# Four layers of a small convolution net on one core: two casts side by side, the last mix in its own bank, the order around the normalisations, and output in four pieces

## The chip, the cores and the metric

The kernel runs on one core of a Trainium2 chip. The metric is the device time of one launch in microseconds (us), as the median of the runs. Engines are named as in the profile: PE is TensorE (PEld its weight loads), DVE VectorE, ACT ScalarE, POOL GpSimd, SP SyncE, which here issues most of the DMAs. Each engine works through its own queue in order, and semaphores order the engines among one another.

## The reference

x has 8 images of 64 channels and 16x16 pixels, float32. Four layers follow one another.

```python
# L0: attention over the 256 pixels of an image, 8 query/key channels
q = einsum('oc,bcn->bno', Wq, xf) + bq ; k = ... ; v = ... + bv[:, None]
attn = softmax(einsum('bno,bom->bnm', q, k), axis=-1)
out = einsum('bcj,bij->bci', v, attn)
x = gamma * (einsum('oc,bcn->bon', Wo, out) + bo[:, None]) + x
# L1: the same without Wo: x = x + out
# L2: pre-activation block with one-bit weights
wq(w) = mean(abs(w)) * sign(w)
out = relu(batch_norm(x, gamma0, beta0))     # statistics over images and pixels
out = conv3x3(out, wq(w0))
out = relu(batch_norm(out, gamma1, beta1))
x = conv3x3(out, wq(w1)) + x
# L3: whitening of the four quarters of the channels against one another
xc = x - mean ; cov = einsum('cqn,cpn->cqp', xc, xc) / N        # 4x4 for each of 16 channels
U = cholesky(cov + EPS * eye(4)).T ; z = solve_triangular(U, xc)
out = einsum('pqc,qbchw->pbchw', weight, z) + bias
```

## The kernel before

The 128 partitions hold two images of 64 channels (g = 0, 1), so the 8 images are 4 pairs of 256 columns each (PAIRS = 4, N = 256). The two attention layers are 8 iterations i = 0..7, one for each pair and layer. Nothing is scheduled by a planner: the order on every engine is written out by hand as a list of calls, and each call names the semaphores that it waits for.

One iteration of attention, by the names of its steps: project(i) makes queries and keys on PE (fp32, bank to bank); first_parts(i) copies them into cut with the bias (DVE), later_parts (DVE, for i = 0) or parts1/parts2 (POOL) split them into parts that bf16 can hold; replicate(i) multiplies by half, which adds the parts up along the rows, queries (o = 0) into columns 0 to 255 and keys (o = 1) into columns 256 to 511 of pb_rep; queries_keys(i) casts the 512 columns into qk (DVE). scores(i) fills pb_s, maxima (DVE) and totals/logs (ACT) find each row's shift, shifts(i) splits it (POOL), shifts_to_rows(i), shift_rows (ACT), scores_t and add_shifts make the transposed scores with the shifts in them, exps(i) (ACT) the probabilities. values(i) and values_out(i) (DVE) give vt, and mix(i) multiplies probabilities and values. add_shortcut(i) (DVE) adds x. For the last pair, mix(7) does that itself: it puts base = x + bias into its bank first by a product with the identity. keep_warm(count) are products of constants that nobody reads; they keep PE occupied.

Then the normalisation: statistics(b) and the last bn_stats L1144 (DVE), combine(n, ...) on PE, which puts the statistics of both images together, bn_aggr L1185 (DVE), Ln and Exp for rstd (ACT). power_of_two(n) is five dependent operations on one or two columns that turn gamma and beta into values scaled by a power of two. Of layer n = 0, zn of pair 0 is made on DVE and of pair 1 on POOL (L441). Each pair's input to the convolution is two fp16 tiles hi and lo: for pairs 0 and 1 ACT writes hi from zn (L603) and DVE act32 (first_line) and lo (first_low); for pairs 2 and 3 ACT writes act32 (L611) and DVE hi and lo (later_inputs). conv_steps runs the 9 taps of hi and lo of two pairs beside each other, the second five steps (LEAD) behind the first. conv0_statistics(q) are the bn_stats of its results, then comes combine(1, ...). tap_values(n) (POOL) scales the signs of the weights. The means of the absolute weights go from wabs through the matmul L934 into emean and esq.

The tail: yc (the second convolution and the shortcut, DVE), transposed(q), yt (ACT, four copies), gram(q), and on DVE the sums over the masks: cov_q. Two small products with the sums (L976, L978) and the one with cov_q (L980) give the 4x4 matrices, tt is matrix minus means beside the weights of L3. The elimination goes over the pivots on DVE, three operations for each after the first; POOL raises the pivots to the power -1/2 (L459 two of them together, L462, L465), ACT scales the rows by two of them (hot01), DVE makes final_w. The last matmuls (L992) fill four banks, ACT and DVE copy them into res with the bias, SP stores two halves of 256 KB.

## Time and profile before

| What | Value |
|---|---|
| median of 3 runs | 70.03 us (70.02, 70.03, 71.75) |
| profiled execution, its own time | 70.26 us |
| span of that execution, first to last instruction | 68.5 us |
| busy, share of the span | PE 59.2 us (86%), DVE 47.7 (70%), ACT 41.9 (61%), POOL 21.8 (32%) |
| mean granted TensorE clock | 0.990 |
| output stores | 2 of 256 KB, 2.1 us to landing |
| input loads of x | 4 of 128 KB, 2.8 us to landing |

The times are of whole executions; the span is about 1.8 us shorter than the profiled execution's own time. All times of rows are microseconds from the start of the span. No engine is busy all the time, and PE's share has the keep_warm products in it (88 matmuls, 12.3 us), so the shares say little on the end: what counts at each place is the wait that ends last. Small operations on DVE start a little before the one ahead of them has ended, where they don't wait for it.

### The profile page before, as it was taken

To read this page: it belongs to the slowest core of one execution; us is meant where nothing else is said; L and a number is where in the kernel's file an instruction comes from. 1 tells how busy PE (TensorE), PEld (TensorE's weight loads), DVE (VectorE), ACT (ScalarE), POOL (GpSimd) and SP (SyncE) were. 2 spreads that over 40 slices of the span, in tenths; PEclk is the share of its full clock that TensorE was granted. 3 is DMA by queue.
4 is the path that set the end of the run, shared out by engine and by line. 5 is a ranking of instruction groups with operands and counts; after the bars stand their busy time and mean duration, and the time that the engine had idled before them with its cause. 6 is when DMAs were issued, how large, how long until landed. Compare 5 with 4: busy or idle time off the path is not lost. (4 is left out here: it accounts for less than half of the span.)

```text
span 68.5 us, 2099 instructions
## 1 busy us (share of the span) xinstructions
PE 59.2 (86%) x785; PEld 37.1 (54%) x785; DVE 47.7 (70%) x129; ACT 41.9 (61%) x133; POOL 21.8 (32%) x59
## 2 busy tenths in 40 slices
PE   5989888889899989958795999889999999999900
PEld 3325333656555628433362678378885997775400
DVE  0038999595949898994988765778859969266440
ACT  0710098999997699789995682563018573365430
POOL 4000944530545508680303035650004050008100
PEclk9999999999999999999999999999999999999996
DMA  0987940000000000000000000000000000000025
GB/s 0 253 249 186 317 197 0 0 10 0 0 0 0 5 0 0 10 5 0 5 0 0 0 10 0 0 0 10 0 0 0 10 0 0 10 0 0 0 105 201
DMA packets 2169, 2.71 MB, mean 40 GB/s; under 512 B 368, under 2 KB 1520, under 8 KB 2160
## 3 DMA queue, kind: packets, MB, share of 16 engines
q1 hardware_dynamic: 1872, 2.39, 11.0%
q10 hardware_dynamic: 288, 0.20, 0.9%
q8 instruction: 6, 0.10, 0.6%
q14 instruction: 3, 0.02, 0.1%
HBM read 2.06 MB, written 0.52 MB: 38 GB/s over the span
## 5 line engine op out<-in xcount | busy, mean ns | idle before, releaser
L500 ACT ACTIVATE bank<-bank,negmax 128x256 f32<-128x256 f32 x32 | 14.5, 457 | 5.3 <-DVE negmax L1031 5.1
L672 PE MATMUL bank<-const-bfloat16-1.0 128*64 128x512 bf16 x88 | 12.3, 415 | 0.8 <-PEq L1333 0.8
L1031 DVE TENSOR_REDUCE negmax<-bank 128x2 f32<-128x512 f32 x16 | 10.6, 686 | 1.7 <-PE bank L727 1.6
L520 ACT ACTIVATE probs<-bank 128x512 f32<-128x512 f32 x16 | 8.8, 603 | 1.1 <-PE bank L751 1.1
L788 PE MATMUL bank<-probs,vt 128*64 128x256 f32 x64 | 8.9, 386 | 0.3 <-DVE cut L1041 0.3
L893 PE MATMUL bank<-hi,taps 64*64 64x225 f16 (+2 forms) x144 | 7.3, 267 | 0.7 <-ACT hi L603 0.5
L672 PEld LDWEIGHTS bank<-const-bfloat16-1.0 128*64 128x64 bf16 x88 | 5.0, 117 | 4.4 <-issue 1.6
L1041 DVE TENSOR_SCALAR cut<-bank,prm 128x256 f32<-128x256 f32 x8 | 3.8, 481 | 5.1 <-PE bank L683 5.1
L893 PE MATMUL bank<-lo,taps 64*64 64x225 f16 (+2 forms) x144 | 7.0, 265 | 0.0
L893 PEld LDWEIGHTS bank<-hi,taps 64*64 64x64 bf16 x144 | 6.0, 107 | 1.7 <-issue 0.8
L354 POOL TENSOR_TENSOR cut<-cut 64x256 f32<-64x256 f32 x7 | 4.3, 612 | 8.3 <-DVE cut L1041 5.4
L500 ACT ACTIVATION_READ_ACCUMULATOR bank<-bank,negmax 128x1 f32 x32 | 6.9, 215 | 0.0
L893 PEld LDWEIGHTS bank<-lo,taps 64*64 64x64 bf16 x144 | 6.4, 107 | 0.0
L683 PE MATMUL bank<-x,aw 128*64 128x256 f32 x32 | 6.0, 468 | 0.2 <-DMA x<-x_in 0.2
L788 PEld LDWEIGHTS bank<-probs,vt 128*64 128x64 f32 x64 | 5.2, 136 | 1.6 <-issue 0.8
L1055 DVE CAST qk<-bank 128x512 bf16<-128x512 f32 x8 | 5.5, 685 | 0.7 <-PE bank L697 0.7
L370 POOL TENSOR_TENSOR shift<-negmax,lntot 128x4 f32<-128x4 f32 x8 | 1.6, 203 | 11.2 <-issue 9.7
L361 POOL TENSOR_TENSOR cut<-cut 32x256 f32<-32x256 f32 x7 | 4.3, 610 | 0.5
L766 PE MATMUL bank<-half,shift 128*64 128x128 f16 x32 | 2.4, 226 | 2.2 <-POOL shift L377 1.5
L528 ACT ACTIVATE shift_t<-bank 128x256 bf16<-128x256 f32 x8 | 3.1, 386 | 1.8 <-PE bank L766 1.8
L766 PEld LDWEIGHTS bank<-half,shift 128*64 128x64 bf16 x32 | 1.4, 108 | 4.5 <-POOL shift L377 3.9
L683 PEld LDWEIGHTS bank<-x,aw 128*64 128x64 f32 x32 | 2.0, 159 | 3.4 <-DMA x<-x_in 2.2
(132 smaller groups left out, 104.9 us busy)
## 6 DMA issues: line engine op xcount, KB each, us to landing
cw<-conv_w SPq DMA_DIRECT2D x2, 288.0 KB, 4.2
x<-x_in SPq DMA_DIRECT2D x4, 128.0 KB, 2.8
out<-res SPq DMA_DIRECT2D x2, 256.0 KB, 2.1
kst<-consts SPq DMA_DIRECT2D x1, 428.0 KB, 5.2
aw<-attn_w ACTq DMA_DIRECT2D x1, 128.0 KB, 2.5
aw<-attn_w SPq DMA_DIRECT2D x1, 128.0 KB, 3.4
half<-select SPq DMA_DIRECT2D x1, 96.0 KB, 2.8
kst<-consts SPq DMA_DIRECT2D x1, 64.5 KB, 3.5
```

The lines of the kernel that those rows point to most:

```text
L354: nc.gpsimd.tensor_tensor(some, some, tops(some), ALU.subtract).then_inc(part1_out, 1)
L361: nc.gpsimd.tensor_tensor(some, some, tops(some), ALU.subtract).then_inc(part2_out, 1)
L500: nc.scalar.activation(part, part, ACT.Exp, bias=negmax[:, i % 2, n:n + 1], accum_out=total[:, i % 2, n:n + 1]).then_inc(total_out, 1)
L520: nc.scalar.activation(probs[:, i % 2, g], pb_t[g][:].rearrange("p (t n) -> p t n", t=CH), ACT.Exp).then_inc(exp_out, 1)
L672: mm(bank[lanes(h)], filler[:, lanes(h)], filled, start=True, stop=True)
L683: last = mm(proj(i)[lanes(h)], aw[:, w + h * C:w + (h + 1) * C], x_of(i), start=True, stop=True)
L766: last = mm(pb_rows[lanes(h), u * P:(u + 1) * P], tops[:, u, P * h + 1:P * (h + 1):2], half[:, 0, :], start=True, stop=True)
L788: last = mm(mixed(i)[g * C:(g + 1) * C], vt[:, i % 2, t, g * C:(g + 1) * C], probs[:, i % 2, g, t, :], start=(t == 0 and i < ITERS - 1), s ...
L893: last = mm(img(pb_conv[n][q][lanes(to), 0:N])[:, kept(dy, H), kept(dx, W)], taps[n][lanes(g), tap, :], (hi, lo)[part][n][lanes(g), q, shi ...
L1031: ve.tensor_reduce(negmax[:, i % 2, g * CH:(g + 1) * CH], pb_s[(2 * i + g) % 3][:].rearrange("p (t n) -> p t n", t=CH), AX.X, ALU.max, neg ...
L1041: ve.tensor_scalar(cut[:, i], proj(i), prm[:, bias:bias + 1], None, ALU.add).then_inc(part0_out, 1)
L1055: ve.tensor_copy(qk[:, i].rearrange("p o n -> p (o n)"), pb_rep[:]).then_inc(qk_out, 1)
```

## The change

On the start: power_of_two(0) is called first on DVE; replicate(0) stands ahead of project(2), and one keep_warm is dropped; for i = 0 the keys go into pb_s[2] and ACT casts them (semaphore k0_out), DVE casts the 256 columns of queries. At attention's end: the shortcut of the last pair is issued in last_shortcut() after mix(4), into pb_rep, and mix(7) adds to it there; power_of_two is no longer called behind statistics(0). Around the normalisation: the weight means' matmuls stand behind combine(0, ...) and their steps on emean and esq behind first_low; zn of pair 1 is made on DVE; power_of_two(1) is called behind later_inputs(0, 3), ahead of conv0_statistics(0), and tap_values(1) on POOL after the first scale and shift. In the tail: the fourth yt copy goes to DVE; WARM[4] is 1 in place of 3 and stands behind the matmuls L976 and L978; the powers are taken one by one, the first already from the matrix (a_out), the last one on ACT as exp(k ln p); in the elimination the product no longer waits for the reciprocal, which goes into the last operation; the output is made and stored in four pieces of 128 columns of two pairs, 128 KB each.

```diff
-WARM = (4, 6, 2, 4, 3, 15)
+WARM = (4, 6, 2, 4, 1, 15)
-WARM_START = (6, 1, 5, 4)
+WARM_START = (6, 5, 4)
...
-        pb_out = pb_conv[1]
+        pb_out = [[banks[n] for n in ns] for ns in ((6, 7), (4, 5), (2, 0), (6, 7))]
+        PIECES = tuple((k, first) for k in (0, 2) for first in (0, P))
-        pb_q = banks[0]
+        pb_q = banks[1]
...
-            return pb_pv[:, 0:N] if i < ITERS - 1 else pb_v[:, 0:N]
+            return pb_pv[:, 0:N] if i < ITERS - 1 else pb_rep[:, 0:N]
...
+            for n in range(len(PIECES)):
+                sp.wait_ge(res_act, n + 1)
+                sp.wait_ge(res_dve, n + 1)
+                sp.dma_start(out[:, quarter(n)], res[:, quarter(n)]).then_inc(stored, 16)
...
             tap_values(0)
-            tap_values(1)
             for n in range(2):
                 pool.wait_ge(var_out, n + 1)
-                if n == 0:
-                    nc.gpsimd.tensor_scalar(zn[0][:, 1], xs[LAYERS][:, quarter(1)], mv[0][:, 0:1], bn_t[0][:, 4:5],
-                                            ALU.subtract, ALU.mult).then_inc(z_pool, 1)
...
+                if n == 0:
+                    tap_values(1)
...
+            def power(j):
+                nc.gpsimd.tensor_tensor(roots[:, j:j + 1], pivot[:, j:j + 1], kst[:, K_EXPO + j:K_EXPO + j + 1],
+                                        ALU.pow).then_inc(root_out, 1)
+                pool.wait_ge(root_out, j + 1)
+            pool.wait_ge(a_out, 1)
+            power(0)
+            for j in range(1, Q - 1):
+                pool.wait_ge(pivot_out, j)
+                power(j)
...
             first_bias()
+            act.wait_ge(rep_mm, 1)
+            nc.scalar.activation(qk[:, 0, 1], pb_s[2][:, 0:N], ACT.Identity).then_inc(k0_out, 1)
...
-            for q in range(PAIRS):
+            for q in range(PAIRS - 1):
                 act.wait_ge(yt_mm, q + 1)
...
+            act.wait_ge(pivot_out, Q - 1)
+            nc.scalar.activation(lnp[:], tt[:, Q - 1, Q - 1:Q], ACT.Ln).then_inc(lnp_out, 1)
+            act.wait_ge(lnp_out, 1)
+            nc.scalar.activation(piv[:], lnp[:], ACT.Exp, scale=kst[:, K_EXPO + Q - 1:K_EXPO + Q]).then_inc(piv_out, 1)
...
+                        to = pb_s[2][lanes(h), 0:N] if i == 0 and o == 1 else pb_rep[lanes(h), o * N:(o + 1) * N]
...
+            def last_shortcut():
+                pe.wait_ge(base_out, 1)
+                pe.wait_ge(id_in, 16)
+                pe.wait_ge(qk_out, ITERS)
+                for h in range(2):
+                    mm(mixed(ITERS - 1)[lanes(h)], ident[:, lanes(h)], base[:], start=True, stop=False,
+                       skip_group_check=True)
...
             project(0)
             project(1)
+            replicate(0)
             project(2)
-            keep_warm(WARM_START[1], pb_t[0])
-            replicate(0)
             project(3)
             scores(0)
...
             mix(4)
+            last_shortcut()
             shifts_to_rows(6, 6)
...
+            pe.wait_ge(x_out, ITERS - 1)
+            pe.wait_ge(stats0_out, PAIRS - 1)
+            combine(0, range(PAIRS - 1))
+            pe.wait_ge(last_stats, 1)
+            combine(0, range(PAIRS - 1, PAIRS))
             pe.wait_ge(wabs_out, 2)
             for n in range(2):
                 last = mm(pb_mean[:, n:n + 1], kst[:, K_ONES:K_ONES + P], wabs[n][:],
                           start=True, stop=True)
             last.then_inc(e_mm, 1)
...
-            keep_warm(WARM[4])
-
             pe.wait_ge(sum_out, 1)
             mm(pb_means[:, 0:Q], kst[:, K_REP:K_REP + P], sum_q[:], start=True, stop=True).then_inc(means_mm, 1)
             mm(pb_bias[:, 0:1], kst[:, K_AVG:K_AVG + P], sum_all[:], start=True, stop=True).then_inc(sum_mm, 1)
+            keep_warm(WARM[4])
             pe.wait_ge(cov_out, 1)
...
+            for n, (k, first) in enumerate(PIECES):
                 pe.wait_ge(zc_out, k + 2)
+                if n == 3:
+                    pe.wait_ge(res_act, 1)
+                    pe.wait_ge(res_dve, 1)
                 for g in range(G):
                     for half_out in range(2):
+                        at = (k + half_out) * N + first
+                        last = mm(pb_out[n][g][lanes(half_out), 0:P], weights[lanes(g)],
+                                  zc[lanes(g), at:at + P], start=True, stop=True)
...
+                if i == 0:
+                    ve.tensor_copy(qk[:, 0, 0], pb_rep[:, 0:N]).then_inc(qk_out, 1)
...
+            power_of_two(0)
             first_parts(0)
...
             statistics(0)
-            power_of_two(0)
-            power_of_two(1)
             values_out(6)
...
-                for q in range(1 + n):
+                for q in range(2):
...
                     first_low(0, 1)
+                    dve.wait_ge(e_mm, 1)
+                    step(ve.tensor_copy(emean[:], pb_mean[:, 0:2]))
+                    step(ve.tensor_tensor(esq[:], emean[:, 0:1], emean[:, 0:1], ALU.mult))
                     step(ve.tensor_scalar(esq[:], esq[:], E_SQUARE_MIN, None, ALU.max))
                     later_inputs(0, 2)
                     step(ve.reciprocal(einv[:], esq[:]))
                     later_inputs(0, 3)
+                    power_of_two(1)
                     conv0_statistics(0)
...
+            dve.wait_ge(yt_mm, PAIRS)
+            ve.tensor_copy(yt[:, 6:8], pb_yt[3][:, 0:2 * P].rearrange("p (k g c) -> p k g c", k=2, g=G)).then_inc(yt_dve, 1)
...
-                step(ve.reciprocal(inv[:, j:j + 1], tt[:, j, j:j + 1]))
-                step(ve.scalar_tensor_tensor(some, row, inv[:, j:j + 1], lij, ALU.mult, ALU.mult))
-                ve.tensor_tensor(below, below, some, ALU.subtract).then_inc(pivot_out, 1)
+                ve.scalar_tensor_tensor(some, row, -1.0, lij, ALU.mult, ALU.mult).then_inc(dve_step, 1)
+                ve.reciprocal(inv[:, j:j + 1], tt[:, j, j:j + 1]).then_inc(dve_step, 1)
...
+                ve.scalar_tensor_tensor(below, some, inv[:, j:j + 1], below,
+                                        ALU.mult, ALU.add).then_inc(pivot_out, 1)
```

## Rows read from the trace of the kernel before

**Rows 1.** Chain of waits in order of time: start us, us, what
```profile
40.09 0.43 PE bank L783 x4
...
41.38 0.54 PE bank L934 x4
...
43.48 1.38 POOL zn L441
```

**Rows 2.** Timeline, first pair: start us, us, engine line op, [idle before it <- releaser]
```profile
3.35 1.12 PE L683 MATMUL bank<-x,aw 128*64 128x256 f32 x4
...
3.44 0.30 ACT L477 ACTIVATE gbo<-prm 128x1 f32<-128x1 f32 x1 [0.52 <-DMA prm<-params]
...
5.56 0.42 DVE L1050 TENSOR_TENSOR cut<-cut 32x256 f32<-32x256 f32 x1
...
6.29 0.39 PE L697 MATMUL bank<-cut,half 128*64 128x256 bf16 x4
...
6.64 0.65 PE L683 MATMUL bank<-x,aw 128*64 128x256 f32 x4
...
7.47 0.39 PE L727 MATMUL bank<-qk 64*128 64x256 bf16 x4 [0.18 <-DVE qk L1055]
```

**Rows 3.** Timeline, end of attention
```profile
33.99 0.30 PE L766 MATMUL bank<-half,shift 128*64 128x128 f16 x4 [0.47 <-POOL shift L377]
...
34.85 0.14 DVE L1012 TENSOR_REDUCE bn_t<-prm 128x1 f32<-128x2 f32 x1
...
36.56 0.20 POOL L377 TENSOR_TENSOR shift<-shift 128x4 f32<-128x4 f32 x1
...
36.63 0.23 DVE L1018 TENSOR_SCALAR bn_t<-prm,bn_t 128x2 f32<-128x2 f32 x1
...
36.89 0.42 DVE L1061 COPY vt<-bank 128x256 f32<-128x256 f32 x1
...
37.42 0.30 PE L766 MATMUL bank<-half,shift 128*64 128x128 f16 x4 [0.75 <-POOL shift L377]
...
40.99 0.28 DVE L1141 COPY tt<-prm 128x16 f32<-128x16 f32 x1
...
41.42 0.43 DVE L1144 BATCH_NORM_STATS2 stats<-bank 128x6 f32<-128x256 f32 x1
```

**Rows 4.** Timeline, first normalisation and its end
```profile
42.92 0.38 DVE L1185 BATCH_NORM_AGGREGATE mv<-bank 128x2 f32<-128x48 f32 x1 [0.51 <-PE bank L868]
...
47.95 0.43 DVE L1176 BATCH_NORM_STATS2 stats<-bank 128x6 f32<-128x256 f32 x1
...
49.71 1.13 PE L868 MATMUL bank<-stats,kst 128*128 128x18 f32 x8
```

**Rows 5.** Timeline, covariance to output
```profile
59.91 0.18 DVE L1236 TENSOR_TENSOR cov_q<-cov,kst 128x16 f32<-128x16 f32 x1
...
60.40 0.38 PE L980 MATMUL bank<-cov_q,kst 128*128 128x16 f32 x2
...
60.86 0.17 DVE L1247 TENSOR_TENSOR tt<-bank,dd 128x16 f32<-128x16 f32 x1
...
61.68 0.73 POOL L459 TENSOR_TENSOR root<-tt,kst 128x2 f32<-128x2 f32 x1 [5.41 <-DVE tt L1258]
...
61.76 0.23 DVE L1264 SCALAR_TENSOR_TENSOR upd<-tt,inv 128x12 f32<-128x12 f32 x1
...
62.49 0.57 POOL L462 TENSOR_TENSOR root<-tt,kst 128x1 f32<-128x1 f32 x1
...
63.78 0.28 DVE L1274 SCALAR_TENSOR_TENSOR final_w<-kst,piv,coef 128x64 f32<-128x64 f32 x1
...
64.82 0.91 ACT L648 ACTIVATE res<-bank,prm 128x256 f32<-128x256 f32 x2 [0.95 <-PE bank L992]
...
65.46 0.82 SPq L339 DMA_DIRECT2D out<-res  x2
```

**Rows 6.** DMA issues: KB each, median us from issue to landing
```profile
out<-res SPq DMA_DIRECT2D x2, 256.0 KB, 2.1
```

More of the change, by code:

```diff
@@ L317, in shifted, with result @@
             return slice(max(0, d), size + min(0, d))
+        def result(n, g):
+            first = n * N + g * P
+            return res[:, first:first + P]
         def img(ap):
@@ L644, in _ @@
                                      bias=dmean[:]).then_inc(zc_out, 1)
-            for k in range(0, PAIRS, 2):
-                act.wait_ge(fin_mm, k + 1)
-                nc.scalar.activation(res[:, k], pb_out[k][:, 0:N], ACT.Identity,
+            for n in range(len(PIECES)):
+                act.wait_ge(fin_mm, 2 * n + 1)
+                nc.scalar.activation(result(n, 0), pb_out[n][0][:, 0:P], ACT.Identity,
                                      bias=prm[:, P_BIAS3:P_BIAS3 + 1]).then_inc(res_act, 1)
@@ L696, in replicate @@
                     for h in range(2):
-                        last = mm(pb_rep[lanes(h), o * N:(o + 1) * N], half[:, 1 + o, lanes(h)], tops(cut[:, i]),
+                        to = pb_s[2][lanes(h), 0:N] if i == 0 and o == 1 else pb_rep[lanes(h), o * N:(o + 1) * N]
+                        last = mm(to, half[:, 1 + o, lanes(h)], tops(cut[:, i]),
                                   start=True, stop=True)
@@ L777, in mix @@
                         pe.wait_ge(x_out, i)
-                else:
-                    pe.wait_ge(rows_out, ITERS)
-                    pe.wait_ge(base_out, 1)
-                    pe.wait_ge(id_in, 16)
-                    for h in range(2):
-                        mm(mixed(i)[lanes(h)], ident[:, lanes(h)], base[:], start=True, stop=False,
-                           skip_group_check=True)
                 for g in range(G):
@@ L936, in _ @@
             last.then_inc(e_mm, 1)
-            pe.wait_ge(x_out, ITERS - 1)
-            pe.wait_ge(stats0_out, PAIRS - 1)
-            combine(0, range(PAIRS - 1))
-            pe.wait_ge(last_stats, 1)
-            combine(0, range(PAIRS - 1, PAIRS))
             keep_warm(WARM[1], pb_q)
@@ L986, in _ @@
             weights = final_w[:].rearrange("p q j -> p (q j)")
-            for k in range(0, PAIRS, 2):
+            for n, (k, first) in enumerate(PIECES):
                 pe.wait_ge(zc_out, k + 2)
+                if n == 3:
+                    pe.wait_ge(res_act, 1)
+                    pe.wait_ge(res_dve, 1)
                 for g in range(G):
                     for half_out in range(2):
-                        last = mm(pb_out[k + g][lanes(half_out), 0:N], weights[lanes(g)],
-                                  zc[lanes(g), quarter(k + half_out)], start=True, stop=True)
+                        at = (k + half_out) * N + first
+                        last = mm(pb_out[n][g][lanes(half_out), 0:P], weights[lanes(g)],
+                                  zc[lanes(g), at:at + P], start=True, stop=True)
                     last.then_inc(fin_mm, 1)
@@ L1178, in _ @@
             for n in range(2):
-                if n == 0:
-                    dve.wait_ge(e_mm, 1)
-                    step(ve.tensor_copy(emean[:], pb_mean[:, 0:2]))
-                    step(ve.tensor_tensor(esq[:], emean[:, 0:1], emean[:, 0:1], ALU.mult))
                 dve.wait_ge(comb_mm, n + 1)
@@ L1276, in _ @@
                                     ALU.mult, ALU.mult).then_inc(fw_out, 1)
-            for k in range(1, PAIRS, 2):
-                dve.wait_ge(fin_mm, k + 1)
-                ve.tensor_scalar(res[:, k], pb_out[k][:, 0:N], prm[:, P_BIAS3:P_BIAS3 + 1], None,
+            for n in range(len(PIECES)):
+                dve.wait_ge(fin_mm, 2 * n + 2)
+                ve.tensor_scalar(result(n, 1), pb_out[n][1][:, 0:P], prm[:, P_BIAS3:P_BIAS3 + 1], None,
                                  ALU.add).then_inc(res_dve, 1)
```

69 lines of the change are left out of this document (32 added, 37 removed).

## The prediction

> **What bounds the kernel now.** I read the chain of waits in order of time first, since no engine is busy throughout: it passes from engine to engine, so only work that stands on it counts. Three pieces of it are what the change is about: four matmuls that put the shortcut into the last pair's bank, the matmuls of the weight means (L934) ahead of the statistics' matmuls, and a 1.38 us normalisation on POOL [rows 1]. Then I read the timeline of the four stretches that the edits touch, to see at each place which wait ends last once the present one is gone. The sum is made against the profiled execution (70.26 us, span 68.48 us) and then carried to the median of the runs, 70.03 us, which lies 0.23 us lower.
>
> **Start: replicate(0) ahead of project(2), cast on two engines.** Today replicate(0) begins at 6.29 although the last part of cut is ready at 5.98, and scores(0) begin at 7.47, just behind the cast of 512 columns on DVE [rows 2]. Afterwards replicate(0) can start 0.06 us behind the part, at 6.04. Its two passes take half of its 0.39 us row, so PE is free at 6.26. Now project(2), until now done in the idle time before 5.98, comes behind it. Four such fp32 passes advance PE by 0.43 us (the four shortcut matmuls of the same size, [rows 1]), so project(2) holds it to 6.69 and project(3) (its input is there when it starts at 6.64 today, [rows 2]) to about 7.15. The casts end earlier: replicate's results stand at 6.43 (6.04 + 0.39), a copy of 256 columns out of PSUM takes 0.42 us on DVE [rows 3], DVE is done with cut(1) at 6.5, and ACT is idle. So the cast ends near 6.95, PE's queue is late next, and scores(0) start at 7.15: -0.32 us. Without the move PE would have waited for the cast; with it half of what the split cast could give is spent on project(2). ACT's first exponentials follow these scores, and nothing later in attention waits for a load, so I carry the 0.32 to the end. The bounds are 0 (PE held up, or an engine further on that absorbs it) and 0.5 (project(2) costs nothing). power_of_two(0), five dependent small operations, moves into DVE's idle start. The two calls together take from 34.85 to 36.86 [rows 3], 1.0 us each. Params have landed at 3.44 and DVE's first other work waits for project(0), which ends at 4.47 [rows 2], so it ends at 4.45 and costs nothing. If params came 0.2 us late it would cost 0.1 to 0.2.
>
> **End of attention: power_of_two off DVE.** POOL has the last pair's shifts ready at 36.76, but shifts_to_rows(7) starts at 37.42, because it also waits for v_out of pair 6, whose copy starts at 36.89, right behind the two calls [rows 3]. With the calls gone the copy is done before 36.3. The POOL result is next, and PE starts at 36.82: -0.60 us. All of the last pair's work hangs on it.
>
> **Last mix in its own bank.** The shortcut's 0.43 us leave the chain [rows 1]. They are issued after mix(4) instead, where PE waits for POOL's shifts anyway (0.47 us idle at 33.99, the bracket of that row in [rows 3]), so I cost them at nothing there; if that gap were gone they would cost 0.43. PE alone would gain 0.60 + 0.43, but DVE's own queue is late next: the tt copy starts at 40.99 and takes 0.28, which puts the last bn_stats at 40.62 and not at 41.42 [rows 3], -0.80 us. Its end is then 41.05.
>
> **Order of the statistics' matmuls.** Behind the last bn_stats stand today L934 (0.54 us of the chain, [rows 1]) and the full eight matmuls of combine. In the new order the four for the first three pairs are done before, and only four are left. Eight take 1.13 us [rows 4] and each advances by 0.11, so four take 0.69 with the latency. bn_aggr starts at 41.05 + 0.06 + 0.69 = 41.80 in place of 42.92 [rows 4]: -1.12 us.
>
> **Normalisation: given back in part.** zn of pair 1 moves from POOL (1.38 us, [rows 1]) to DVE, 0.41 us there as for pair 0. That frees ACT's second hi and with it the second half of the convolution's start by more than 1.5 us. But then DVE has everything: from bn_aggr it needs, one behind the other, two zn, two lines, two lows, the two small steps on emean that stood ahead before, the maximum, then hi and lo of pairs 2 and 3. With 0.34 us from start to start for 256-column operations and 0.19 for small dependent ones, lo of pair 3 starts at 46.14. Then comes power_of_two(1), 1.0 us. The first bn_stats of the convolution starts at 47.51, against 47.95 [rows 4], only 0.44 us sooner. By the same spacings the third starts 1.08 us later and ends at 49.02, the fourth at 49.36. The convolution itself is over at about 48.3, 2.1 us behind hi of pair 3. So PE waits here, 0.8 us, for DVE. combine(1) starts at 49.07 and not at 49.71 [rows 4] and runs its eight matmuls without a further gap in 1.05 to 1.13: -0.70 us at the second bn_aggr (bounds -0.5 if the small operations go slower, -1.45 if DVE were no bound). tap_values(1) waits on POOL for power_of_two(1) until 47.3; behind it in POOL's queue stand only the scale and shift of the second normalisation, needed at 50.5, and its taps are ready at 48.1. The second convolution is unchanged and all of it moves with this.
>
> **Tail, up to the weights.** The covariance matmul L980 starts at 60.40, although cov_q is complete at 60.09: the mean matmuls and three pairs of fillers stand ahead of it [rows 5]. With these ahead of the fillers and one pair left, it starts at 60.14: -0.26, and dd is ready before it. Fourth yt on DVE: the gram matmuls run without a gap and would ask for it at 58.9; the copy ends at 58.7, no gain and no cost. Next, the pivots. The DVE steps per pivot are three either way, one of them now without a wait: nothing. The powers go one by one from the first matrix on instead of from the first elimination. POOL takes 0.73 us for two values, 0.57 for one [rows 5]. The first starts 0.15 behind the tt of 60.60 + 0.18, at 60.94, and three of 0.57 with 0.08 between end at 62.80, against 63.06 for root2. The last pivot goes through ACT: Ln and Exp of one value from 62.5 on, at most 0.30 each as for gbo [rows 2], end by 63.2 and are not waited for. final_w starts at 63.39 to 63.42 and not at 63.78 [rows 5]: -0.38 with the 0.26 in it, so -0.12 for the powers (bounds 0, if a single first power costs 0.73, and -0.2).
>
> **Four pieces out.** The first results come sooner: the first copy starts 0.48 us behind PE's start and not 0.70 (64.82, [rows 5]), and a copy of 128 columns ends after an estimated 0.35 instead of 0.47 (two of 256 in 0.91, with some fixed part). So the first issue falls 0.98 us behind PE's start instead of 1.34. But four issues follow at 0.45 us, the time of an issue on SP now (two in 0.82, the second waiting on a copy, [rows 5]), so the last is issued 2.33 behind and not 1.78. It carries a quarter and finds the queue empty. A 256 KB transfer lands in 2.1 us [rows 6], of which about 0.35 goes by halving it and 0.1 by the empty queue, so 1.62: 3.95 behind PE's start against 3.98 now, no gain. Bounds: -0.2 and +0.5. [...]
>
> **Sum.** -0.32 - 0.70 - 0.26 - 0.12 - 0.03 = -1.43 us: 70.26 becomes 68.83, the median of 70.03 becomes 68.6. What a measurement of this kernel can tell from no change is about 2%, that is 68.63, so the forecast lies on the line.
>
> **Rivals.** (1) DVE is no bound in the first convolution: PE then gains 1.45 in place of 0.70, 67.9 us. Against it: the count of operations above. (2) The ends don't pay: scores(0) start no earlier, because POOL's parts of pair 1 or the loads rule, and four issues cost 0.3 us more than two. 68.6 + 0.32 + 0.3 = 69.2 us. For it: PE's idle time before 5.98 was covered by project(2), and the last issue is 0.55 us later behind PE's start. (3) DVE and POOL block each other in the pivots. Today DVE's update at 61.76, both inputs in SBUF, ran in 0.23 us beside the power of 61.68 to 62.41 [rows 5], so I give it little. If each power held up a DVE step, the pivots would go in turns and final_w would be 0.6 us later, 69.2 us. This is what the Trainium skill says, SBUF — State Buffer (Who interferes with whom): a DVE instruction with two SBUF inputs and a GpSimd one that reads SBUF exclude each other for the whole instruction; by that rule the update would not have ended before 62.6, and the trace has it end at 61.99. (4) Slower than before: the matrix clock comes up later. The first project takes 1.12 us and the fourth 0.65 for the same work [rows 2], though the granted clock shown is 0.9 or more throughout: PE starts at its lower level (1.2 GHz) and has 2.4 GHz by the fourth. The change leaves PE idle from 5.6 to 6.04 and drops a filler there. One of the three runs took 71.75, 1.72 more than the median; if that is a late rise and becomes the rule, the result is 68.6 + 1.72 = 70.3 us. It decides from 1.43 us on, when the added time is more than all the gains.
>
> **How the numbers follow.** Forecast 68.6: 0.58; (1) 0.11; (2) 0.20; (3) 0.05; (4) 0.06. The range must leave out at most 0.2: it goes from 68.0, the edge of (1), to 69.5, which holds (2) and (3) and leaves (4) outside. Over 2% faster: 0.34 of the forecast's 0.58 and all of (1), 0.45. Slower by over 2%, over 71.4, only if the clock stays low still longer: 0.03. Within 2%: 0.52.
>
> **What would show it.** In the profile of the changed kernel: scores(0) about 0.3 us earlier with PE and not DVE ahead of them; shifts_to_rows(7) directly behind POOL's shift; the shortcut's matmuls near 33 us; the first bn_aggr 1.4 to 1.5 us sooner than 42.92; PE idle near 48 us, waiting for bn_stats; the second bn_aggr 1.0 sooner; final_w 1.4 sooner; four issues 0.45 us apart at the end. I am wrong if the idle gap ahead of combine(1) is missing, if PE's clock falls in it (it would nearly double the second convolution), or if a single power costs as much as two.

## The result and the profile after

Measured: 69.14 us median (69.05 to 69.25 in four runs) against 70.03 for the kernel before on the same chip, ratio 0.988 [0.986, 0.990]. The forecast was 68.6. The profiled execution has its own time of 69.05 us and a span of 67.3 us, against 70.26 and 68.48: 1.21 us less in its own time. Most kernels here, the one before too, also have some executions 1.2 us or more longer, and ratios and comparisons leave those out.

The timeline of the changed kernel's first pair (start us, us, engine, line, operation; in brackets the idle time before it and its releaser):

```profile
5.97 0.42 PE L710 MATMUL bank<-cut,half 128*64 128x256 bf16 x4 [1.05 <-DVE cut L1073]
...
6.22 1.03 PE L694 MATMUL bank<-x,aw 128*64 128x256 f32 x8
6.43 0.38 ACT L540 ACTIVATE qk<-bank 128x256 bf16<-128x256 f32 x1 [2.64 <-PE bank L710]
6.43 0.42 DVE L1079 CAST qk<-bank 128x256 bf16<-128x256 f32 x1
...
7.18 0.39 PE L742 MATMUL bank<-qk 64*128 64x256 bf16 x4
```

Both halves of the cast are over at 6.85, yet scores(0), L742, start only at 7.18 and show no wait: the eight matmuls of project(2) and project(3) hold PE. Against 7.47 in [rows 2] that is 0.29 us. Of these, 0.07 are no work of the edits: the last part of cut was ready at 5.91 here (the new order starts replicate(0) 0.06 us behind it, at 5.97) and at 5.98 in the kernel before. Next the end of attention and the first normalisation, same columns:

```profile
33.51 0.30 PE L781 MATMUL bank<-half,shift 128*64 128x128 f16 x4
...
36.33 0.30 PE L781 MATMUL bank<-half,shift 128*64 128x128 f16 x4
...
39.90 0.28 DVE L1166 COPY tt<-prm 128x16 f32<-128x16 f32 x1
40.09 0.42 DVE L1169 BATCH_NORM_STATS2 stats<-bank 128x6 f32<-128x256 f32 x1
...
41.31 0.38 DVE L1205 BATCH_NORM_AGGREGATE mv<-bank 128x2 f32<-128x48 f32 x1 [0.80 <-PE bank L885]
...
41.72 0.74 DVE L1210 TENSOR_SCALAR zn<-x,mv,bn_t 128x256 f32<-128x256 f32 x2
...
44.08 0.16 DVE L1221 TENSOR_TENSOR esq<-emean 128x1 f32<-128x1 f32 x1
...
47.02 0.43 DVE L1201 BATCH_NORM_STATS2 stats<-bank 128x6 f32<-128x256 f32 x1
...
48.66 0.37 PE L885 MATMUL bank<-stats,kst 128*128 128x18 f32 x2 [0.90 <-DVE stats L1201]
```

shifts_to_rows(6) and (7), now L781, come at 33.51 and 36.33 where they were at 33.99 and 37.42 [rows 3]: 0.48 us sooner before the edits to the end of attention, so 0.19 more than the start gave, and 1.09 after them; the last bn_stats stands right behind the tt copy; bn_aggr is 1.61 us sooner than in [rows 4]. Ahead of it the eight matmuls of combine run from 40.13 without a pause, the last pair's four from 40.57, when their bn_stats has been over for 0.06 us: DVE's queue and PE's end together here. The last row is the new wait: the convolution on PE is over and PE idles 0.90 us for DVE's statistics. The chain of waits (start us, us, what) says the same, since between bn_aggr and that point it runs through DVE alone; a few of its pieces:

```profile
46.08 0.07 DVE bn_t L1035
...
46.75 0.24 DVE bn_t L1041
...
47.02 0.43 DVE stats L1201
```

bn_t L1035 to L1041 is power_of_two(1), on the path from 46.08 to 47.0. The tail in the timeline:

```profile
58.98 0.39 PE L999 MATMUL bank<-cov_q,kst 128*128 128x16 f32 x2
...
59.47 0.17 DVE L1272 TENSOR_TENSOR tt<-bank,dd 128x16 f32<-128x16 f32 x1 [0.27 <-PE bank L999]
59.79 1.83 POOL L464 TENSOR_TENSOR roots<-tt,kst 128x1 f32<-128x1 f32 x3 [4.68 <-DVE tt L1272]
59.90 0.24 DVE L1284 SCALAR_TENSOR_TENSOR tt<-tt,upd 128x21 f32<-128x21 f32 x1
...
62.24 0.28 DVE L1303 SCALAR_TENSOR_TENSOR final_w<-kst,piv,coef 128x64 f32<-128x64 f32 x1
...
62.69 0.89 PE L1015 MATMUL bank<-zc,final_w 64*64 64x128 f32 x24
...
63.68 1.83 SPq L346 DMA_DIRECT2D out<-res  x4
```

L1015 starts 0.17 us behind the end of final_w (62.52), with no wait of its own: the last fillers hold PE. In the view of DMA issues (KB each, median us from issue to landing) a quarter of the output lands only 0.3 us sooner than the half of [rows 6]:

```profile
out<-res SPq DMA_DIRECT2D x4, 128.0 KB, 1.8
```

### The profile page after: what moved, and what is told of

Its sections match the earlier page's. It is cut to its first block and busy times, and to the rows that moved or that the text cites. A ratio compares the mean times of both kernels' runs of the same rounds, so it can differ in the third digit from the quotient of the medians.

```text
span 67.3 us, 2133 instructions
## 1 busy us (share of the span) xinstructions
PE 57.7 (86%) x795; PEld 36.7 (54%) x795; DVE 48.0 (71%) x133; ACT 42.5 (63%) x137; POOL 20.0 (30%) x58
## 5 line engine op out<-in xcount | busy, mean ns | idle before, releaser
L683 PE MATMUL bank<-const-bfloat16-1.0 128*64 128x512 bf16 x82 | 11.5, 418 | 0.8 <-PEq L1362 0.8
L694 PE MATMUL bank<-x,aw 128*64 128x256 f32 x32 | 5.2, 421 | 0.1
L1081 DVE CAST qk<-bank 128x512 bf16<-128x512 f32 x7 | 4.8, 684 | 0.5 <-PE bank L710 0.5
L710 PE MATMUL bank<-cut,half 128*64 128x256 bf16 x32 | 3.4, 284 | 1.5 <-DVE cut L1073 1.0
L1087 DVE COPY vt<-bank 128x256 f32<-128x256 f32 x8 | 3.4, 422 | 1.4 <-PE bank L726 1.4
```

The costliest lines, as they stand in the source:

```text
L683: mm(bank[lanes(h)], filler[:, lanes(h)], filled, start=True, stop=True)
L694: last = mm(proj(i)[lanes(h)], aw[:, w + h * C:w + (h + 1) * C], x_of(i), start=True, stop=True)
L710: last = mm(to, half[:, 1 + o, lanes(h)], tops(cut[:, i]), start=True, stop=True)
L1081: ve.tensor_copy(qk[:, i].rearrange("p o n -> p (o n)"), pb_rep[:]).then_inc(qk_out, 1)
```

## Experiments

Times of variants of the changed kernel are best read against a fellow run on the same chip, and marks inside a profile from its own scores(0), since scores(0) moved by 0.4 us between two executions of the same kernel (7.47 and 7.89 in the kernel before).

**The kernel before, once more.** No edit. 

> The kernel before, unchanged, for a second profiled execution. Theory: the first one held a chance stall of about 0.2 to 0.3 us on ACT (at 23.27, where ACT waited 0.2 us with its input ready), so that this one comes nearer to the median of the runs: span 68.2 to 68.3, and the exponentials of pair 4 start 0.2 us sooner in it. Rival: the stall belongs to the kernel and the changed kernel took it away; then the span is 68.5 again with the same wait.

Measured: 70.75 us, span 68.9. ACT again stands still for 0.23 us with nothing it waits for, so it was no chance of one execution: the rival holds, and the longer span comes from scores(0), which start at 7.89 here and at 7.47 there. The stall is taken up under "one more instruction".

**Two stores.**

```diff
-            for n in range(len(PIECES)):
-                sp.wait_ge(res_act, n + 1)
-                sp.wait_ge(res_dve, n + 1)
-                sp.dma_start(out[:, quarter(n)], res[:, quarter(n)]).then_inc(stored, 16)
+            for n in range(0, len(PIECES), 2):
+                sp.wait_ge(res_act, n + 2)
+                sp.wait_ge(res_dve, n + 2)
+                sp.dma_start(out[:, n * N:(n + 2) * N], res[:, n * N:(n + 2) * N]).then_inc(stored, 16)
...
```

> The changed kernel with its four pieces stored by two DMAs of 256 KB instead of four of 128 KB. Theory (four issues in a row are what lost the tail's gain): first issue at 63.94, second at 64.71 in place of the fourth at 65.10; both land within 2.0 to 2.1, so the span ends about 0.2 us sooner: 68.9. Rival (the landing of small stores is what costs, or the copies): no gain or a loss, since the first store starts 0.27 us later; 69.1 to 69.3.

Measured: ratio to before 0.978 [0.971, 0.984], from two runs, 68.89 and 69.19. That can't be told from the changed kernel by time. The profile can: with two issues SP is done sooner behind PE's start, though each moves twice the bytes.

```profile
64.22 0.89 PE L1015 MATMUL bank<-zc,final_w 64*64 64x128 f32 x24
...
65.47 1.10 SPq L346 DMA_DIRECT2D out<-res  x2
```

The issues end at 66.57, 2.35 us behind PE's start, and those of the changed kernel at 65.51, 2.82 behind; a half then lands 2.0 us behind the start of its issue and a quarter 1.8. What both come to is the stretch from the start of the final matmuls to the end of the span: 4.39 us here and 4.58 in the changed kernel. The same stretch is 4.57 to 4.60 us in all seven profiles with four stores, 4.39 in both with two stores and four copies, and 4.36 in the kernel before. Four stores lose 0.2 us against two, and cutting the output into four pieces gains nothing over the two of before.

**Thirteen pairs of fillers instead of fifteen** ahead of the final matmuls (the last entry of WARM). 

> The changed kernel with 13 instead of 15 pairs of fillers ahead of the last matmuls. Theory (the last fillers, which end at 62.6, hold back the final matmuls, whose weights are ready at 62.52): these start at 62.58 instead of 62.69, 0.1 us sooner, 69.0. Rival (0.17 us is simply the time that PE needs after final_w): no change. A clock that falls for want of fillers would show as slower final matmuls, +0.3 us or more.

Measured: ratio 0.978 [0.972, 0.984], from 69.04, 69.05 and 69.12. In the profile the hold-up goes; the matmuls now start 0.06 us behind the end of final_w and show a wait for it:

```profile
63.81 0.28 DVE L1303 SCALAR_TENSOR_TENSOR final_w<-kst,piv,coef 128x64 f32<-128x64 f32 x1
...
64.15 0.89 PE L1015 MATMUL bank<-zc,final_w 64*64 64x128 f32 x24 [0.25 <-DVE final_w L1303]
```

**power_of_two(1) early**, back into attention, but far ahead of its end: at about 19 us, before add_shortcut(1), where DVE waits anyway.

```diff
             maxima(3, 1)
+            power_of_two(1)
             add_shortcut(1)
...
                     later_inputs(0, 3)
-                    power_of_two(1)
```

> The changed kernel with power_of_two(1) moved from between the convolution's inputs and its statistics to DVE's 0.87 us of idle time before add_shortcut(1). Theory (those five operations on DVE hold back combine(1) by 0.9 us): PE's idle time of 0.9 us ahead of combine(1) goes, the fourth bn_stats is gated by the convolution (47.8), the second bn_aggr starts at 48.9 in place of 49.7, and the run takes 68.3 to 68.5. Rival (attention has no room for 1.0 us on DVE: add_shortcut(1) and what follows is late by 0.15 us or more and carries on): 68.5 to 69.0. If the convolution's end rather than DVE bounds, no gain.

Measured: ratio 0.972 [0.968, 0.977], from 68.50 to 68.86. combine(1) starts without a wait at 48.01 and the second bn_aggr at 49.18, 0.54 us sooner, of which 0.12 are an earlier scores(0) (7.06 against 7.18). From the first bn_aggr to the second it is 7.90 us against 8.41. So DVE was the bound of the first convolution, power_of_two(1) stood on its path, and PE is the bound now. It is less than the expected 0.8, and the time lies in the range of the rival, but what the rival names is not seen: the first bn_aggr comes 34.22 us behind scores(0), against 34.13 in the changed kernel and 34.24 in the variant with two stores. One part of the difference shows in the timeline:

```profile
43.19 1.30 POOL L428 TENSOR_SCALAR taps<-sign,bn_t 128x576 bf16<-128x576 f32 x1
44.06 0.43 DVE L1222 TENSOR_TENSOR esq<-emean 128x1 f32<-128x1 f32 x1
...
48.01 1.13 PE L885 MATMUL bank<-stats,kst 128*128 128x18 f32 x8
```

tap_values(1) runs as soon as its power is there, and now falls beside DVE's work. It takes 1.30 us instead of 0.74, and the product of one value per partition on DVE, 0.16 us in the changed kernel (L1221), takes 0.43 and ends with it. This is what the Trainium skill says in SBUF — State Buffer (Who interferes with whom): a DVE instruction that reads two inputs from SBUF and a GpSimd one that reads SBUF shut each other out. The trace agrees with it for the product, but not throughout: the two lows (L1188, at 43.21 and 43.55), whose inputs are both in SBUF, take 0.41 us each beside the same tap_values(1), which had started at 43.19, and no more than in the changed kernel. In the pivots the trace doesn't agree either: L1284, with two inputs from SBUF, takes 0.24 us beside the first power, which runs from 59.79 to 60.35. For which pairs of operations the rule holds stays open.

**Both power_of_two calls moved, on the kernel before.**

```diff
-            power_of_two(0)
-            power_of_two(1)
             values_out(6)
...
+            power_of_two(0)
             first_parts(0)
...
             maxima(3, 1)
+            power_of_two(1)
             add_shortcut(1)
```

> The kernel before with one part of the change alone: power_of_two(0) in front of first_parts(0), power_of_two(1) in DVE's idle time before add_shortcut(1). Theory: shifts_to_rows(7) starts 0.6 us sooner (0.05 us behind POOL's shift) and everything behind it moves with it, so the median is 0.6 us under that of the kernel before. Rival (the wait for the shift or DVE's other work takes its place): under 0.3 us.

Measured: ratio 0.992 [0.988, 0.995], 0.6 us. In the timeline the copy of vt no longer stands behind the two calls, and the matmuls wait for POOL alone:

```profile
36.21 0.42 DVE L1061 COPY vt<-bank 128x256 f32<-128x256 f32 x1 [0.87 <-PE bank L713]
...
36.97 0.20 POOL L377 TENSOR_TENSOR shift<-shift 128x4 f32<-128x4 f32 x1
...
37.23 0.30 PE L766 MATMUL bank<-half,shift 128*64 128x128 f16 x4 [0.16 <-POOL shift L377]
```

That execution's scores(0) came 0.31 us late, so 37.23 stands for 36.92: 0.50 us against [rows 3]. From shifts_to_rows(6) to (7) it is 2.83 us in place of 3.43, a gain of 0.59. The 0.10 between the two is lost near 15 us, before power_of_two(1) runs at 19.5, and the variant with two stores shows it too, so it is no price of the move.

**The last mix in its own bank, on the kernel before**, and its shortcut matmuls behind mix(4). The fillers that used banks[0] go to banks[1], as in the changed kernel.

```diff
-            return pb_pv[:, 0:N] if i < ITERS - 1 else pb_v[:, 0:N]
+            return pb_pv[:, 0:N] if i < ITERS - 1 else pb_rep[:, 0:N]
...
             mix(4)
+            last_shortcut()
             shifts_to_rows(6, 6)
```

> The kernel before with one edit: the last mix in its own bank and its four shortcut matmuls behind mix(4). Theory (PE's chain loses the 0.43 us, then DVE's own queue is next): the last mix is done near 40.93 instead of 41.36, but the tt copy stands ahead of the last bn_stats on DVE from 40.99 on and lets it start 0.19 us behind, at 41.18 instead of 41.42: -0.24 us there and at every later mark, median 69.8 us, ratio 0.997; shifts_to_rows(7) not later than 37.42 if the shortcut's matmuls fit the 0.47 us gap. Rival A (all of the 0.43 arrives): last bn_stats at 40.99, median 69.6. Rival B (the shortcut's matmuls do not fit the gap near 34 and push PE): L766 of pair 7 up to 0.4 us later and nothing gained.

Measured: ratio 0.996 [0.993, 1.000], that is 0.25 us. The timeline:

```profile
34.32 0.30 PE L766 MATMUL bank<-half,shift 128*64 128x128 f16 x4
...
37.75 0.30 PE L766 MATMUL bank<-half,shift 128*64 128x128 f16 x4 [0.76 <-POOL shift L377]
...
41.32 0.28 DVE L1144 COPY tt<-prm 128x16 f32<-128x16 f32 x1
41.51 0.42 DVE L1147 BATCH_NORM_STATS2 stats<-bank 128x6 f32<-128x256 f32 x1
...
42.82 0.38 DVE L1188 BATCH_NORM_AGGREGATE mv<-bank 128x2 f32<-128x48 f32 x1 [0.40 <-PE bank L871]
```

This execution is 0.30 us late at scores(0) and 0.33 at both shifts_to_rows: 34.32 and 37.75 against 33.99 and 37.42. So the moved matmuls cost nothing, and L766's gap of 0.47 in [rows 3] is filled. Less that 0.33, bn_stats comes 0.24 us sooner, 0.19 behind the tt copy, as the theory had it. But bn_aggr comes 0.43 sooner (42.49 against 42.92). What was wrong is the step after it: between the last mix and bn_aggr it is PE's queue that is late, L934 and the eight matmuls, and not the last bn_stats. The whole 0.43 arrives at bn_aggr, and counted from scores(0) 0.39 of it stand at the end of the span, as rival A had it, though by another way. The interval of the time reaches from 0 to 0.5 us and can't tell the theory's 0.24 from it.

**zn of pair 1 back on POOL, in the changed kernel.**

```diff
                 pool.wait_ge(var_out, n + 1)
+                if n == 0:
+                    nc.gpsimd.tensor_scalar(zn[0][:, 1], xs[LAYERS][:, quarter(1)], mv[0][:, 0:1], bn_t[0][:, 4:5],
+                                            ALU.subtract, ALU.mult).then_inc(z_pool, 1)
...
-                for q in range(2):
+                for q in range(1 if n == 0 else 2):
...
```

> The changed kernel with the normalisation zn of pair 1 back on POOL, ahead of the scale and shift there. Theory (DVE is late everywhere between bn_aggr and the first bn_stats, so what counts is what DVE waits for): zn on POOL ends 1.38 us behind 41.72, near 43.10; hi of pair 1 on ACT moves from 42.76 to about 43.16, the second line and low on DVE by 0.2 us, scale and shift on POOL by 0.7 us (43.83 in place of 43.12), ACT's pieces of pairs 2 and 3 by 0.65 us, which DVE's casts have slack for except the first. First bn_stats of the convolution 0.15 to 0.25 us later than 47.02, median 69.3 us. Rival (DVE's queue is the bound by its count of operations, and one operation of 0.33 us fewer makes it earlier): first bn_stats 0.1 to 0.3 us sooner, median 68.9 us. Rival 2 (the move of zn is what gave the 2 us at hi of pair 1 and the kernel needs them): 0.5 us or more slower, 69.7 us.

Measured: 69.54 to 69.72, ratio 0.991 [0.988, 0.994]: 0.5 us over the changed kernel's 69.14, which was taken on another chip, and 0.3 over the next variant, on the same chip, which lacks the gain of the start. From the first bn_aggr to the first bn_stats it takes 6.18 us (42.68 to 48.86), against 5.71 in the changed kernel: 0.47. That is the size of rival 2; my theory had 0.2:

```profile
43.23 1.37 POOL L446 TENSOR_SCALAR zn<-x,mv,bn_t 128x256 f32<-128x256 f32 x1 [1.70 <-DVE mv L1210]
...
44.63 0.41 DVE L1185 TENSOR_SCALAR act<-zn,rstd,bn_t 128x256 f32<-128x256 f32 x1 [0.57 <-POOL zn L446]
44.69 0.60 ACT L615 ACTIVATE hi<-zn,bn_t,rstd 128x256 f16<-128x256 f32 x1 [0.47 <-POOL zn L446]
```

I had left out that POOL starts 0.14 us later than DVE would, and that the second lo waits for this hi. The move pays though it adds to the engine that is the bound there.

**The start undone, in the changed kernel.**

```diff
+            project(2)
+            keep_warm(WARM_START[1], pb_t[0])
             replicate(0)
-            project(2)
...
-            act.wait_ge(rep_mm, 1)
-            nc.scalar.activation(qk[:, 0, 1], pb_s[2][:, 0:N], ACT.Identity).then_inc(k0_out, 1)
...
```

> The changed kernel with the start alone as it was before: replicate(0) behind project(2) and one filler, one cast of 512 columns on DVE; power_of_two(0) stays in the start and everything else stays. Theory (the start's 0.32 us, of which the trace of the changed kernel showed 0.29, goes through to the end): scores(0) at about 7.47 us if the matrix clock rises as early as in the profile of before, all later marks 0.3 us later, and the median 0.3 us over that of the changed kernel, 69.4 us, ratio to before near 0.992. Rival A (the early replicate causes the late rises of the clock that the changed kernel's records showed at 10.2 us in one profile): then the times near 70.5 us vanish with it and all runs lie near 69.4. Rival B (the 0.29 is absorbed before the end of attention): median unchanged at 69.1.

Measured: ratio 0.987 [0.983, 0.992], from two runs, 69.42 and 69.33, 0.2 us over the changed kernel's median, which was taken on another chip. It points to the start's gain coming through, and doesn't show it. The other three took 70.82, 71.32 and 72.48, so the times over 70.5 don't vanish with the early replicate: rival A falls. The profile shows that the gain of the start is no fixed number. Here is project(1), which waits for x(1), and scores(0), first with the old order:

```profile
5.32 1.25 PE L692 MATMUL bank<-x,aw 128*64 128x256 f32 x8 [0.75 <-DMA x<-x_in]
...
7.80 0.39 PE L737 MATMUL bank<-qk 64*128 64x256 bf16 x4 [0.36 <-DVE qk L1074]
```

and with the new one, in the variant with two stores, where x(1) lands as late:

```profile
5.28 0.65 PE L694 MATMUL bank<-x,aw 128*64 128x256 f32 x4 [1.13 <-DMA x<-x_in]
...
7.21 0.39 PE L742 MATMUL bank<-qk 64*128 64x256 bf16 x4
```

That is 0.59 us, twice the 0.29 of the two main profiles: in the old order project(1) and project(2) stand ahead of replicate(0), and x(1) landed early in the profile of the kernel before (project(1) starts at 4.66).

**One more instruction on ACT, in the kernel before**, behind gbo, where ACT is idle:

```diff
             first_bias()
+            nc.scalar.activation(spare[:], prm[:, P_BO:P_BO + 1], ACT.Identity).then_inc(spare_set, 1)
             totals(0, 0)
```

> The kernel before with one added instruction: ACT scales nothing and writes one value per partition into a spare tile, directly behind gbo, some 5 us before its first exponentials, where ACT is idle. Nothing reads it. Background: in the profiles of before and of each variant without ACT's share of the first cast, ACT stands still for 0.23 to 0.25 us behind its cast of shift_t near 23 us, with nothing that it waits for; in the profiles of all kernels with that cast it doesn't. Theory (what counts is the position of the instructions in ACT's program: one more at the start shifts the place where it stalls): the idle time of 0.23 behind that shift_t is gone, nothing else is changed in the program, and the first bn_aggr comes 0.15 to 0.2 us sooner, measured from scores(0): median 0.2 us less than before, ratio 0.997. Rival A (the stall comes from something else in the variants, the order of PE's or DVE's work at the start, or the place of the tiles): the 0.23 stays, ratio 1.000. Rival B (the stall moves to another place on ACT's path): the 0.23 is gone there and a like gap stands elsewhere, ratio 1.000.

Here is the place in the kernel before:

```profile
22.66 0.38 ACT L528 ACTIVATE shift_t<-bank 128x256 bf16<-128x256 f32 x1 [0.85 <-PE bank L766]
23.27 0.45 ACT L500 ACTIVATE bank<-bank,negmax 128x256 f32<-128x256 f32 x1 [0.23 <-issue]
```

and with the added instruction:

```profile
22.86 0.38 ACT L529 ACTIVATE shift_t<-bank 128x256 bf16<-128x256 f32 x1 [0.85 <-PE bank L768]
23.16 0.45 ACT L501 ACTIVATE bank<-bank,negmax 128x256 f32<-128x256 f32 x1
```

The stall is gone. The first bn_aggr comes at 43.02, with scores(0) at 7.66: 0.09 us sooner from there than before. The time, ratio 0.998 [0.995, 1.002], can't show so little. The changed kernel has just such an added instruction, ACT's half of the first cast. In the eight profiles with it the stall is absent, in the five without it (the kernel before twice, both power_of_two moved, own bank, start undone) it is present. Why the place in ACT's program matters is not shown.

**PE's clock: the changed kernel again, and kept warm.** The second edit puts fillers into both idle stretches:

```diff
             project(0)
+            keep_warm(1, pb_t[0])
             project(1)
...
+            keep_warm(4)
             pe.wait_ge(eps1_set, 1)
```

> The changed kernel, unchanged, beside the other kernels of this group. Theory (the two groups of times seen in its relatives, near 69.0 and near 70.3, belong to it too and come from PE's clock): some runs near 69.1, some near 70.3 with a mean granted clock below that of the fast ones or a rise of the clock after 6 us. Rival (they came from the edits in those relatives): all runs within 0.3 us of 69.1.

> The changed kernel with fillers in PE's two idle times: one pair between project(0) and project(1), four pairs ahead of combine(1), where PE waits 0.9 us for DVE. They lie in waits, so the fast runs stay at 69.1 (up to 69.3 if the first pair delays project(1)). Theory (the clock's late rise at the start and its fall behind the second wait make the runs near 70.3): none or few of those are left. Rival (the slower runs have another cause): as many of them as in the changed kernel.

Measured: the changed kernel again, 69.14 and 69.21, and 70.52, 70.63 and 70.72. The first two give a ratio of 0.981 [0.977, 0.986], 1.3 us, where the main comparison gave 0.84: the size of the gain is known to some 0.5 us only. With the fillers four runs, 69.26 to 69.59, and none near 70.5. They aren't free: these times are 0.1 to 0.4 us over those of the changed kernel, and in the profile combine(1) starts 0.08 us later, counted from scores(0). The profile that the repeat left is that of the 70.52, and the timeline of its first matmuls tells why:

```profile
5.12 1.12 PE L694 MATMUL bank<-x,aw 128*64 128x256 f32 x4 [0.57 <-DMA x<-x_in]
...
6.54 1.91 PE L694 MATMUL bank<-x,aw 128*64 128x256 f32 x8
8.39 0.61 PE L742 MATMUL bank<-qk 64*128 64x256 bf16 x4
```

The same eight matmuls take 1.91 us where they take 1.03 above: PE is still at 1.2 GHz, after 0.57 us in which it stood idle because x(1) had not landed. scores(0) come 1.21 us later, and the end 1.47. The pause alone doesn't do it: in the variant with two stores PE waited 1.13 us at this place (the row above) and was at 2.4 GHz behind it, but there it had been before it too, since its first project took 0.73 us and not 1.12. The profiles with 13 fillers and with zn on POOL show the same late rise as this one. No profile was taken of a long execution of the kernel before, so its cause is not shown.

The second kind of long execution has a mean granted clock of 0.973 or 0.974. In the variant with two stores it is in the profile; windows with the busy time of PE, PEld, DVE, ACT and POOL, then the granted clock, DMA share and GB/s:

```profile
50.00:51.00 1.00, 1.00 (x12) 0.37 (x8) 0.96 (x3) 0.63 (x4) 0.12 (x1) 1.00 0.00 0
51.00:52.00 1.00, 0.85 (x10) 0.67 (x10) 0.86 (x3) 1.00 (x3) 0.45 (x3) 0.70 0.00 0
52.00:53.00 1.00, 1.00 (x22) 0.88 (x20) 0.96 (x4) 1.00 (x3) 0.00 (x0) 0.50 0.00 0
```

The clock falls to half (1.2 GHz) in the second convolution, over 2 us behind the 0.90 us in which PE waits for DVE (to 48.79 here). All kernels with that wait (the changed one, two stores, 13 fillers, zn on POOL, start undone) have 7 such runs among 35, three of them in the five with the start undone and one in the nine of the changed kernel itself. Those without it (the kernel before and its variants, the early power, the warmed one and the joined one below) have none among nearly a hundred, but only 13 of these are of kernels with the rest of the change, and at one in five, 13 would show none by chance about once in 18 times. So the new wait seems to have a second price. That it is the gap that brings the fall rests on these counts and two profiles (the other is that of the start undone); it is not shown.

**Joined.** The early power_of_two(1), two stores, 13 fillers, a filler between project(0) and project(1), and tap_values(1) back behind tap_values(0), out of DVE's way. 

> Power_of_two(1) in DVE's idle time before add_shortcut(1) (68.5 alone), two stores of 256 KB, 13 pairs of fillers at the end, tap_values(1) back behind tap_values(0), and one pair of fillers between project(0) and project(1). Theory: tap_values(1) on POOL ran at 43.19 beside DVE's small product of emean, which took 0.43 instead of 0.16 us, and all of DVE's chain was 0.25 us late; with it moved away that product takes 0.16 us and the span is 0.25 shorter, two stores give 0.2, the fillers 0.1: 67.9 to 68.0. Rival (the convolution on PE bounds, not DVE): 68.2 to 68.3.

Measured: 68.14 to 68.28, median 68.23, ratio to before 0.968 [0.965, 0.971], the fastest of all and with none longer in four. The expected 67.9 to 68.0 was missed; it is the range of the rival, PE as the bound. Without tap_values(1) beside it the product of one value takes 0.16 us again, and from the first bn_aggr to the second it is 7.63 us against 7.90 with the early power alone, the expected 0.25. PE is the bound: DVE waits for the convolution's last bank, and combine(1) starts at 48.05 right behind the convolution:

```profile
48.08 0.43 DVE L1202 BATCH_NORM_STATS2 stats<-bank 128x6 f32<-128x256 f32 x1 [0.18 <-PE bank L910]
```

## Why the prediction was right, and where it was off

The range held the time, and the direction was right; the forecast was 0.54 us too fast. A part of the sum came out by luck: a stall on ACT that I had not seen went away, worth 0.1 to 0.2 us, and covers some of what the tail lost. By its own terms, in the profiled executions:

| term | forecast | measured |
|---|---|---|
| start, to scores(0) | -0.32 | -0.29 |
| ACT's stall near 23 us | none | -0.09 to -0.19 |
| scores(0) to second bn_aggr, without it | -0.70 | -0.68 to -0.78 |
| covariance matmul | -0.26 | -0.26 |
| powers, to final_w | -0.12 | -0.12 |
| behind final_w | -0.03 | +0.33 |
| sum | -1.43 | -1.21 |

**Start.** Right, with the engine named: PE's queue and not the cast is late. But 0.07 of the 0.29 come from cut being ready sooner, so against the same input the edits gave 0.22 in this pair of profiles: PE needs 1.21 us from replicate(0) to scores(0), and I had 1.11. Where x(1) lands late the edits give more, 0.59. That all of it reaches the end is only indicated.

**End of attention.** power_of_two: -0.60 forecast, -0.59 from shifts_to_rows(6) to (7) where it was moved by itself. Own bank: costed at nothing where it went, and so it was. The step from there was partly wrong in its reason: I let DVE's tt copy limit the gain at the last bn_stats, which is what happens there, but in the kernel before bn_aggr hung on PE's queue: L934 ran from 41.31 beside the last bn_stats (41.42 to 41.85) and not behind it. In the changed kernel both queues end together, so the bn_aggr forecast from DVE's (41.80 less the start's 0.32 and the stall's 0.19, 41.29) meets the 41.31 measured. In the changed kernel, shifts_to_rows(7) gained 0.61 over shifts_to_rows(6), as forecast.

**Normalisation and first convolution.** Right. DVE is the bound: PE's idle time of 0.8 us was forecast and 0.90 measured. Rival (1), DVE no bound, is refuted by PE's wait for DVE and by what moving power_of_two(1) away gains. zn on DVE was on the forecast's path at no net price, and putting it back costs 0.47.

**Tail.** This is the term that failed, by 0.36. Behind final_w, 0.11 of it is the fillers. They stand behind the covariance matmul in PE's queue and move with it, so it is not the earlier time that counts but the length of the stretch that they fill. From the start of that matmul to the end of final_w it was 3.67 us, and fifteen pairs just fitted: the final matmuls started 0.06 us behind final_w. The powers one by one make it 3.54, and now the fillers end last. The early power moves all of this 0.5 us forward once more, and the matmuls stand 0.17 us behind final_w as before. So the 0.12 of the powers was right at final_w, and next to nothing of it came through. Nothing in the sum asked whether the fillers still end in time.

The other 0.25 is in the stores. 0.07 is the fourth issue, 2.40 behind PE's start and not 2.33. 0.18 is the landing: 1.8 us and not 1.62, and most of that is how I reckoned. 2.1 less 0.35 less 0.1 is 1.65, and the 3.98 of today that I compared with is 1.78 and 2.20: the two halves landed in 2.03 and 2.19 us, and I took the longer for today and the median for the change. From 2.19 the same deductions give 1.74; the last quarter took 1.79. Rival (2) was thus half right: four issues cost, and the start paid.

**Rival (3)**, exclusion in the pivots: no. Something like it occurred at another place once tap_values(1) ran beside a product on DVE.

**Rival (4)**, the clock: a late rise is there in three profiles, but not as the rule: the four executions of the main comparison lie within 0.2 us. My price was 1.72, the profile shows +1.47. A fall of the clock with the gap ahead of combine(1), named as what would make me wrong, comes behind it in some runs, one of nine of the changed kernel.

**From the sum to the median** another 0.32 went: the kernel before was profiled 0.23 above its median and the changed one 0.09 below. Carrying the sum over by a fixed difference takes the profile's own scatter along. On the other chip the same two kernels lie 1.3 us apart, so this part may be scatter alone.

## What to carry to other kernels

When a stretch that fillers bridge gets shorter, even by 0.1 us, count the fillers again: they hold the matmuls behind them without a wait in the profile, and the gain is lost. When work is moved onto an engine, write out its queue up to the next point where another engine waits: that count forecast PE's gap here, 0.8 us for 0.90 measured, and it also says which small steps to move elsewhere. Half the bytes in a transfer don't take half the time off, and each further issue takes SP another 0.45 to 0.50 us here.

## Not expected of the hardware

- ACT stood still for 0.23 us at one place of its program. One instruction more, 20 us earlier, removed it; 0.09 us were gained at the first bn_aggr.
- A pause of 0.90 us in PE's work ahead of the second convolution went with a fall of the granted clock to 0.5 in 7 of 35 runs, and none was seen where the pause was filled or absent.
- A product of one value per partition on DVE took 0.43 us beside a POOL operation of 576 columns, and 0.16 otherwise; POOL's went from 0.74 to 1.30. Two operations of 256 columns with both inputs in SBUF kept their 0.41 us beside the same POOL operation.
- A 128 KB transfer landed in 1.8 us and one of 256 KB in 2.0 to 2.1.
